# Where the B and C rows of a selective scan are spread over the partitions: by TensorE and ScalarE, or by DMA from DRAM

## The reference, cut to what matters

```python
proj = jnp.einsum('kbcl,kcd->kbld', xs, x_proj_w)
dpart, Bm, Cm = proj[..., :dr], proj[..., dr:dr + N], proj[..., dr + N:]      # N = 16 states
...                                                                           # delta: softplus of a projection of dpart
def step(state, inp):
    d, b, c, uu = inp
    dA = jnp.exp(d[..., None] * A_neg[:, None, :, :])
    state = dA * state + (d * uu)[..., None] * b[:, :, None, :]
    y = jnp.einsum('kbcn,kbn->kbc', state, c)
    return (state, y)
```

## Time and profile before

| | us |
|---|---|
| median of 3 runs | 19,633.7 (19,631.5 to 19,641.2) |
| the profiled execution, its own time | 19,631.1 |
| its span, first to last instruction | 19,629.4 |
| layers 0 and 1, until the first scan of layer 2 | about 6,910 |
| one tile of the scan in layer 2, state cleared to last add to y | 188, 48 times |
| DMA traffic over the span | 562.5 MB, 29 GB/s |

### The profile page before, as it was taken

The page is one execution under the profiler, slowest core; times in us unless marked ns, Lnnn a source line. Parts: engine busy times, 40 slices in busy tenths (PEclk is TensorE's granted clock), DMA queues, the critical chain, the costliest instruction groups (busy, mean ns, idle before and its releaser), DMA issues. The chain is left out here.

```text
span 19629.4 us, 279252 instructions
## 1 busy us (share of the span) xinstructions
PE 15129.9 (77%) x79256; PEld 8976.9 (46%) x79256; DVE 13659.5 (70%) x13058; ACT 9809.7 (50%) x14679; POOL 7610.5 (39%) x4057
## 2 busy tenths in 40 slices
PE   7899998999989767767666767667767767767789
PEld 5666665666666533333333333333333333333367
DVE  5555555555565588787688787688788778887732
ACT  4444444444444366665356666356665446665500
POOL 1000000000000067666366666357666447766500
PEclk9999998999999889999898999889999989999999
DMA  4222222222221200000100000100000100000011
GB/s 112 58 58 52 52 54 61 52 54 55 52 61 47 59 4 3 4 1 3 46 7 4 3 1 3 42 11 4 4 1 3 36 17 4 1 4 3 23 51 39
DMA packets 127667, 562.53 MB, mean 29 GB/s; under 512 B 20988, under 2 KB 81788, under 8 KB 105468
## 3 DMA queue, kind: packets, MB, share of 16 engines
q1 hardware_dynamic: 114780, 470.00, 9.8%
q0 software_dynamic: 12288, 86.71, 2.0%
HBM read 440.00 MB, written 126.27 MB: 29 GB/s over the span
## 5 line engine op out<-in xcount | busy, mean ns | idle before, releaser
L1153 POOL TENSOR_TENSOR L2.u<-L2.u 128x784 f32<-128x784 f32 x3072 | 5657.3, 1849 | 1819.8 <-PE L2.ps L1258 1231.8
L1258 PE MATMUL L2.ps<-L2.u,L2.ident 128*128 128x392 f32 x12288 | 4594.0, 499 | 129.4 <-DVE L2.y L1615 129.4
L1627 DVE TENSOR_TENSOR_SCAN L2.u<-L2.u,L2.state,L2.ps 128x784 f32<-128x784 f32 x2304 | 4164.4, 1835 | 175.4 <-ACT L2.ps L1410 146.7
L1416 ACT COPY L2.u<-L2.ps 128x784 f32<-128x784 f32 x3840 | 3102.9, 808 | 901.5 <-PE L2.ps L1227 894.7
L1227 PE MATMUL L2.ps<-L2.bs,L2.sel 96*128 (+3 forms) x6144 | 1626.3, 352 | 2208.9 <-DVE L2.u L1627 926.2
L1410 ACT ACTIVATE L2.u<-L2.d,L2.nega 128x784 f32<-128x784 f32 x2304 | 2190.8, 951 | 2144.5 <-DVE L2.u L1627 1969.4
L1258 PEld LDWEIGHTS L2.ps<-L2.u,L2.ident 128*128 128x128 f32 x12288 | 2176.7, 192 | 1401.6 <-DVE L2.y L1615 186.1
L1602 DVE TENSOR_TENSOR L2.ps<-L2.ps,L2.du 128x784 f32<-128x784 f32 x2304 | 2216.4, 970 | 717.6 <-PE L2.ps L1227 698.8
L1227 PE MATMUL L2.ps<-L2.cs,L2.sel 96*128 96x392 bf16 (+1 forms) x6144 | 1628.1, 348 | 702.4 <-ACT L2.u L1416 670.0
L1227 PEld LDWEIGHTS L2.ps<-L2.bs,L2.sel 96*128 x6144 | 541.6, 101 | 3073.0 <-issue 2861.3
L1142 POOL TENSOR_TENSOR L2.u<-L2.u,L2.du 128x784 f32<-128x784 f32 x768 | 1410.8, 1837 | 1188.0 <-ACT L2.u L1416 1188.0
(11 more groups left out here) (231 smaller groups left out, 22274.0 us busy)
## 6 DMA issues: line engine op xcount, KB each, us to landing
L0.left<-table SPq DMA_DIRECT2D x48, 1176.0 KB
L0.right<-table SPq DMA_DIRECT2D x48, 1176.0 KB
L1.left<-table SPq DMA_DIRECT2D x48, 1176.0 KB
L1.right<-table SPq DMA_DIRECT2D x48, 1176.0 KB
table<-taps POOLq DMA_DIRECT2D x24, 1176.0 KB, 15.3
L0.wg<-L_w SPq DMA_DIRECT2D x49, 433.5 KB, 3.6
L1.wg<-L_w SPq DMA_DIRECT2D x49, 433.5 KB, 3.5
L0.x_res<-x POOLq DMA_DIRECT2D x8, 2352.0 KB, 13.4
```

Source lines behind the costliest of these rows:

```text
L1153: pool.tensor_tensor(hc[:, n % RING, :], hs[:, n % RING, :], cb[n % RING], ALU.mult)\
L1258: mm = pe.matmul(ps[:, 6 + h, 0:HSPAN], ident[:], hc[:, n % RING, h * HSPAN:(h + 1) * HSPAN], start=(n % STATES == 0), stop=(n % STATES == ...
L1416: act.copy(out.rearrange("p (a n) -> p a n", a=2), ps[:, 4:6, 0:HSPAN]).then_inc(c_out, 1)
L1627: dve.tensor_tensor_scan(hs[:, n % RING, :], a, b, state[:, n:n + 1], ALU.mult, ALU.add).then_inc(scanned, 1)
```

## The change

C rows, and the B rows for GpSimd, no longer pass through TensorE and ScalarE. A DRAM tensor `rows` is added, (B or C, tile, half, state, pixel) in fp32, where half is the lower or upper 64 partitions. When f is complete and the last scan is over, SP stores the B and C rows of f there, 12 DMAs of 16 rows for each pair and direction. In the scan SP issues one DMA per item: it reads the 784 numbers of both halves, each repeated 64 times by a step of 0, into the 128 partitions of `cb` or `bb`. GpSimd waits for these DMAs (`c_in`, one semaphore for each slot of the ring, and `bb_in`) in place of `c_out`; TensorE's `row_item` and ScalarE's `copy_row` with all that calls them are taken out. `cs` is no longer gathered (6 gathers for 12). `bb`, `cb`, `db_pool` lie where they lay.

```diff
+    rows = nc.dram_tensor("rows", (2, 3, 2, STATES, TOK), F32).ap()
 # SP, once for each pair and direction
+                    sp.wait_ge(f_out, it * NCHUNK + NCHUNK)
+                    sp.wait_ge(hc_done, it * (3 * TILE_N) + RING)
+                    for e in range(2):
+                        for kind in range(2):
+                            row = 64 * e + 32 + 16 * kind
+                            for i, half in ((e, 0), (e, 1), (2, e)):
+                                sp.dma_start(rows_dram[kind, i, half], f[row:row + 16, :]).then_inc(rows_out, 16)
...
-                    for dst, row in ((bs, 32), (cs, 48)):
-                        for e in range(2):
-                            for i in range(3):
-                                at = 48 * e + 16 * i
-                                sp.dma_start(dst[at:at + 16, :],
-                                             part[i][64 * e + row:64 * e + row + 16, :]).then_inc(gathered, 16)
+                    for e in range(2):
+                        for i in range(3):
+                            at = 48 * e + 16 * i
+                            sp.dma_start(bs[at:at + 16, :],
+                                         part[i][64 * e + 32:64 * e + 48, :]).then_inc(gathered, 16)
+                    sp.wait_ge(rows_out, it * ROWS_OUT + ROWS_OUT)
...
+                    def row_load(out, kind, i, n, c, done):
+                        at = rows_dram[kind, i, :, n % STATES, bass.ds((c + n // STATES) * SPAN, SPAN)]
+                        sp.dma_start(out, bass.AP(tensor=at.tensor, offset=at.offset,
+                                                  ap=[list(at.ap[0]), [0, 64], list(at.ap[1])])).then_inc(done, 16)
+                    def load_b(c, n, i, q0):
+                        if pooled_before(n):
+                            sp.wait_ge(pool_b, q0 + pooled_before(n))
+                        row_load(bb, 0, i, n, c, bb_in)
+                    def load_span(ti, i, c, last):
+                        n0 = sp.snap((ti * NSPAN + c) * STATES)
+                        q0 = sp.snap((ti * NSPAN + c) * len(POOLED))
+                        for n in range(STATES):
+                            sp.wait_ge(hc_done, n0 + (n + 1))
+                            row_load(cb[n % RING], 1, i, n, c, c_in[n % RING])
+                            if pooled(n + LEAD) and (n + LEAD < STATES or not last):
+                                load_b(c, n + LEAD, i, q0)
+                    for i in range(3):
+                        ti = sp.snap(it * 3 + i)
+                        if i < 2:
+                            load_dt(i + 1)
+                        sp.wait_ge(d_step, ti * (5 * ND) + 5 * ND)
...
+                        with sp.Fori(0, NSPAN - 1) as c:
+                            load_span(ti, i, c, False)
+                        load_span(ti, i, NSPAN - 1, True)
 # GpSimd
-                            pool.wait_ge(c_out, i0 + (item_of_b(n) + 1))
+                            pool.wait_ge(bb_in, q0 * 16 + 16 * (pooled_before(n) + 1))
...
-                                pool.wait_ge(c_out, i0 + (item_of_c(n) + 1))
+                                pool.wait_ge(c_in[n % RING], c0 + 16 * (n // RING + 1))
 # TensorE: the order of a span
                                 if n >= LAG or not first:
                                     share(n - LAG, n0, y0)
-                                if n + 3 < STATES or not last:
-                                    c_row(c, n + 3, i0, last)
 # ScalarE: the order of a span
                                 if not last:
                                     act.copy(state[:, n:n + 1], hs[:, n % RING, SPAN - 1:SPAN]).then_inc(kept, 1)
-                                if n + 2 < STATES or not last:
-                                    copy_c(n + 2, n0, i0, q0, last)
```

More of the change, by code:

```diff
@@ L869, with scan_layer @@
 V_CONV, V_CB, V_G, V_B, V_D, V_DT, V_A, V_END = 0, 9, 10, 11, 12, 16, 20, 84
-def scan_layer(nc, sems, tag, x_in, x_out, ap, z_dram, consts):
+def scan_layer(nc, sems, tag, x_in, x_out, ap, z_dram, rows_dram, consts):
     m = Pool(nc, sems, tag)
@@ L974, in scan_layer @@
         b_ready = m.sem("b_ready")
-        c_ready = m.sem("c_ready")
-        c_out = m.sem("c_out")
+        rows_out = m.sem("rows_out")
+        c_in = [m.sem(f"c_in{s}") for s in range(RING)]
+        bb_in = m.sem("bb_in")
         a_ready = m.sem("a_ready")
@@ L1002, in scan_layer @@
         STEPS, TAPS9, SPLITS, GATES = 10, 9, 8, 5
-        GATHER = 12 * 16
+        GATHER = 6 * 16
+        ROWS_OUT = 12 * 16
         TILE_N = NSPAN * STATES
@@ new lines, in _ @@
+                    sp.wait_ge(rows_out, it * ROWS_OUT + ROWS_OUT)
+                    steady(sp)
+                    def row_load(out, kind, i, n, c, done):
[6 more added lines that the diff above has]
+                        row_load(bb, 0, i, n, c, bb_in)
@@ new lines, in _ @@
+                    for i in range(3):
[3 more added lines that the diff above has]
+                        sp.wait_ge(d_step, ti * (5 * ND) + 5 * ND)
+                        steady(sp)
+                        for n in POOLED:
+                            if n < LEAD:
+                                load_b(0, n, i, sp.snap(ti * (NSPAN * len(POOLED))))
+                        with sp.Fori(0, NSPAN - 1) as c:
+                            load_span(ti, i, c, False)
+                        load_span(ti, i, NSPAN - 1, True)
@@ L1146, in times_c_span @@
                             n0 = pool.snap((ti * NSPAN + c) * STATES)
[L1147 removed]
+                            q0 = pool.snap((ti * NSPAN + c) * len(POOLED))
+                            c0 = pool.snap((ti * NSPAN + c) * (16 * (STATES // RING)))
                             for n in range(STATES):
                                 pool.wait_ge(scanned, n0 + (n + 1 + RING))
[L1150 removed]
+                                pool.wait_ge(c_in[n % RING], c0 + 16 * (n // RING + 1))
                                 pool.wait_ge(y_ready, n0 + (n + 1))
@@ L1155, in times_c_span @@
                                 if pooled(n + LEAD) and (n + LEAD < STATES or not last):
-                                    times_b(c, n + LEAD, i0)
+                                    times_b(c, n + LEAD, q0)
                         for n in POOLED:
@@ L1160, in _ @@
                                 pool.wait_ge(d_step, ti * (5 * ND) + 5 * ND)
-                                times_b(0, n, pool.snap(ti * (NSPAN * ITEMS)))
+                                times_b(0, n, pool.snap(ti * (NSPAN * len(POOLED))))
                         with pool.Fori(0, NSPAN - 1) as c:
@@ L1238, in b_row @@
                             spread(bs, c, n, duo[n % 2][:, BANK:SPAN], BANK, SPAN).then_inc(b_ready, 1)
[L1240 to L1251, removed]
                         def share(n, n0, y0):
@@ L1280, in _ @@
                         first = pe.snap(ti * TILE_N)
-                        i0 = pe.snap(ti * (NSPAN * ITEMS))
                         b_row(0, 0, first)
                         b_row(0, 1, first)
[L1284 to L1288, removed]
                         sum_span(0, True, False)
@@ L1413, in decay @@
                                .then_inc(a_ready, 1)
[L1415 to L1429, removed]
                         def decay_span(c, last):
                             n0 = act.snap((ti * NSPAN + c) * STATES)
-                            i0 = act.snap((ti * NSPAN + c) * ITEMS)
-                            q0 = act.snap((ti * NSPAN + c) * len(POOLED))
                             for n in range(STATES):
@@ L1450, in _ @@
                         decay(0, 1, first)
[L1451 to L1455, removed]
                         for c in range(NSPAN):
@@ L1813, in network @@
                       taps=taps[0] if n == 0 else None, later=(taps[1], tables[1]) if n == 0 else None)
-        scan_layer(nc, sems, "L2", x2, x3, ap, z, consts)
+        scan_layer(nc, sems, "L2", x2, x3, ap, z, rows, consts)
         conv_layer(nc, sems, "L3", x3, out, ap["L3_w"], consts)
```

14 lines of the change are left out of this document (2 added, 12 removed).

## The result

Median 41,264.7 us (41,255.0 to 41,268.2, 4 runs) against 19,636.9 us: 2.10 times as long, interval 2.098 to 2.105, so 21,628 us slower. The forecast was 42,300 us.

What follows compares the result with a forecast made beforehand. VectorE was taken to bound the kernel, TensorE's spreading adding; then two-engine loads would. 19,631 us plus 22,570 (470.2 us a tile x 48) plus 100 between tiles gave 42,300 us, range 39,500 to 48,000.

Steps and rivals of the forecast that it cites:

- VectorE sets the pace, TensorE's spreading adds to it: Layer 2's scan loop: VectorE busy 161.2 of 187.6 us, waiting 14.3 us a tile for TensorE's spreading, 686 us in all.
- Two engines for a load: New row loads: equal shares of both outermost counts, 2 and 128, leave 2 of 16 DMA engines, 64 rows each.
- The price of a load: Each 401,408 B load on two engines at 24.7 GB/s: 8.13 us, 80 in a row per tile, 650.4 us.
- the 7.4 us of start and tail: Per scan tile, beside the 80 loads: first issue, landing, last product, last share, add to y and handovers.
- the two bounds: Total time with a load of 7.47 us, 39,670 us, and with one of 9.98 us, 49,300 us.
- The tile before: One scan tile of the old kernel, memset of state to end of last add to y: taken as 187.6 us.
- TensorE's clock: Stretch between scan tiles: TensorE, mostly idle in the loop, runs slower afterwards; 2 us per tile, 100 us, bounds 0 and 300.
- The stores: Rows to DRAM once per direction, 12 stores, 17 us, hidden beside other work: 0 taken, up to 270 us if uncovered.
- SP's issue: SP's own cost per load in the scan: 0.33 to 0.64 us, hidden under the 8.13 us of transfer.
- the landing times of 25 to 30 us: Sign in the scan: time from issue to landing of cb loads, with four queued.
- the first rival: Sixteen engines carry each scan load, 1.0 us of transfer; VectorE gains up to 14.3 us a tile: 18,950 us, chance 12%.
- The point from which the load decides: Scan loop: a load under 2.2 us isn't felt; above it every 0.1 us costs 384 us.

Runs made afterwards that it cites:

- e3_noload: The changed kernel without its 3840 loads and the waits for them, GpSimd multiplying by a constant view of d; 18,718.5 us, ratio 0.953 to the kernel before.
- e1_halves: The changed kernel with each item loaded by two DMAs of 64 partitions, one per image half, outermost count 64; 18,720.6 us, ratio 0.953 to the kernel before.
- e2_four: The changed kernel with every row stored twice for each image half, so a load has outermost count 4; 26,455.3 us (one run).
- e6_eight: As e1_halves, but the 64 repeats written as (8, 8) with step 0, outermost count 8; 19,019.1 us, ratio 0.965 to the kernel before.
- e4_bonly: The kernel before with only GpSimd's 16 B rows a tile by the two-engine load, C as before; 20,663.7 us, ratio 1.052.
- e7_bonly16: As e4_bonly, but each load is two DMAs of 64 partitions with outermost count 64; 18,973.8 us, ratio 0.966 to the kernel before.

## Why the prediction was right, step by step

**VectorE sets the pace, TensorE's spreading adds to it.** Without spreading of C and pooled B (e3_noload) the loop falls from 187.6 to 168.8 us, VectorE busy 159.6 of it. That run frees TensorE and ScalarE together; that VectorE's direct wait was for TensorE is read from the waits, 14.3 us before and 0.3 in e1_halves.

**Two engines for a load.** Shown three times. By the count: the hardware queue of the earlier trace rows had 114,780 packets. Add 491,520 rows (3840 x 128) and 192 stores of 16 rows and 16 small packets (6144), take away 96 gathers of 32 (3072): 609,372. The page has 617,052, which is 7680 more: 3840 x 2. By the dose: outermost count 2, 4, 8, 64 gave 51, 102, 203 and 192 GB/s, the last (and nearly the one before) held back by what the loop asks for. And by undoing it: e1_halves. The rule of the Trainium skill ("DMA: Bandwidth & Descriptors", "Rules for kernel authors") for unequal counts, which no row of before could show, agrees: the changed kernel has 2 against 128, e2_four 4 against 128, and e6_eight is its case of a leading zero-stride count, 8 against 64.

**The price of a load**, the term that was mis-sized: 8.13 us taken, 7.86 measured, 25.5 GB/s for an engine where the earlier trace rows gave 24.7. With 80 x 7.86 = 628.8 and the 7.4 us of start and tail the tile comes to 636.2, and the first twelve tiles average 638.9 (636.8 to 641.7). The difference of 0.27 us x 3840 = 1037 us equals the forecast's whole error, but that is partly luck. Smaller misses cancel: the tile was 2.7 us longer than this sum (+130 us), the tile before 1.5 us longer than the one that was taken (-73), and the stretch between tiles grew less than allowed for (-67). The bounds were not quite those of the rows: the earlier trace rows has slices of 440 and 461 GB/s above the 430 that was called the best, and the two bounds leave out the 100 us that the forecast adds.

**The tile before** was 187.6 us in the earlier trace rows, but 189.1 on the mean of the first twelve and of all (190.4 to 190.7 in the third and fourth direction): (638.9 - 189.1) x 48 = 21,590 of the 21,628 us.

**TensorE's clock.** The granted clock in the loop is 0.56 of full speed, near the lower of its two levels, 1.2 GHz, where it was 0.95: TensorE has 223 us of busy time in 640 and idles between. The stretch between tiles grew by 1.5 us in the one shown, but by 0.7 us on the mean of all, 33 us in sum, where 2 us each and 100 us had been taken.

**The stores** were hidden, as taken: from the last add of a direction to the memset of the next pass 122.3 us on the mean, 121.8 before, and tile 0 takes as long as tile 1 (639.4 us both, on the mean). The first scan of layer 2 starts 6.8 us later (6916.7 for 6910.0). e2_four shows that 24 stores are no longer covered.

**What was wrong.** SP's issue was not 0.6 us under the load's cover: its median is 7.4 us, so SP itself is held, from the third load of a tile on, and two loads and a part of the third are queued, not three or four. It cost nothing, since all it had to do was the next load, but the landing times of 25 to 30 us that were to show the queue aren't in the records. And the first rival was mis-sized: VectorE's waits for y (8.0 us a tile in the earlier trace rows, 5.1 in e1_halves) and for TensorE (14.3, now 0.3) shrank together, and VectorE's busy time fell by 1.6, so that sixteen engines give 18,720 and not 18,950 us (inside the 18,700 to 19,400 given for it). The point from which the load decides, 2.2 us, was right from above (3.93 us costs as computed), while at 2.03 us e6_eight already loses 300 us against e1_halves.

## What to carry to other kernels

Before a load is moved to the DMA, look at the outermost count of both patterns, as the instruction has them: in these runs the load got the largest number of engines up to 16 that divides both. A broadcast written (2, 64, n) ran on 2 engines at 51 GB/s; written twice as (64, n) it had 16 and moved 192 GB/s, all that the loop asked for. Count the small packets for each DMA in a window to see how many engines it had. With a single buffer add up issue, landing, transfer and use: if the sum is longer than the loop's beat, the load sets the pace, even where its engines are idle part of the time (e4_bonly, 12.15 us against 10.97); if it is shorter, nothing is lost (e7_bonly16).

## What the runs showed of the hardware that was not expected

- An issue on SP holds SP once enough rows are queued. With two engines the first two loads of a tile are issued in 0.55 us each, the third takes 5.38 us and the fourth 7.54 (rows below); the median of all is 7,424 ns, nearly the 7.86 us of a load. With four engines the first four take 0.55 to 0.57 us in tile 1, the fifth 3.31, and the median is 2,181 ns. Both times 128 rows had been issued to each engine when SP was held (2 x 64 and 4 x 32). With eight and sixteen engines nothing shows that SP is held: the medians of 616 and 468 ns are those of loads issued one behind the other from a tile's start. In e4_bonly, two engines and one load at a time, the median is 524 ns.

```profile
7579.12 0.55 SPq L1082 DMA_DIRECT2D L2.u<-rows  x1
...
7581.08 5.38 SPq L1082 DMA_DIRECT2D L2.u<-rows  x1
...
7586.80 7.54 SPq L1082 DMA_DIRECT2D L2.u<-rows  x1
```

- One 3136-byte row read 64 times over is as fast as different rows. 12.9% of 16 x 400 us for 6512 rows is 127 ns a row with two engines, 25.8% of 16 x 100 us for 3251 rows 127 ns with four, 51.6% for 6477 rows 127 ns with eight: 24.7 GB/s of busy time. The different rows give 1.58 MB in 104.1% of 16 x 4 us, 23.7 GB/s. With sixteen it is 177 ns (67.8%, 6131 rows), although the rate in total is no higher. Why is open; no run here reads different rows in this loop.
